# Local attention: the order of the projections, and which PSUM banks they use

## The reference, cut to what matters

```
q, k, v = split(layernorm(x) @ w_qkv.T + b_qkv)      # 16 heads of 16
scores  = q @ k.T / 4, for keys within 16 tokens of the query (window 33)
context = softmax(scores) @ v
x       = x + context @ w_out.T + b_out
```

## Time and profile before

| | us |
|---|---|
| timed runs | 1705.42, 1699.30, 1704.94 |
| their median | 1704.94 |
| the profiled execution | 1711.97 |
| its span, first to last instruction | 1709.9 |

### The profile page before, as it was taken

The page is one execution under the profiler, slowest core; times in us unless marked ns, Lnnn a source line. Parts: engine busy times, 40 slices in busy tenths (PEclk is TensorE's granted clock), DMA queues, the critical chain, the costliest instruction groups (busy, mean ns, idle before and its releaser), DMA issues.

```text
span 1709.9 us, 41993 instructions
## 1 busy us (share of the span) xinstructions
PE 1623.2 (95%) x14962; PEld 1099.3 (64%) x14963; DVE 1146.7 (67%) x2505; ACT 856.6 (50%) x1474; POOL 671.8 (39%) x652
## 2 busy tenths in 40 slices
PE   6999999999989999998999999999999989997999
PEld 3565556666656776765555656666566767776666
DVE  6677765666656666657765556666687677776675
ACT  4355533444376655644344334443466565564774
POOL 2342332334213222232332323444244588888243
PEclk9999999999999999999999999999999999999999
DMA  7132323333301211003210123333332033221011
GB/s 253 50 103 80 104 79 94 110 111 108 86 18 26 37 25 25 1 1 96 84 42 28 42 70 103 111 111 93 93 67 44 7 71 77 58 59 40 14 37 50
DMA packets 90149, 115.69 MB, mean 68 GB/s; under 512 B 9296, under 2 KB 76400, under 8 KB 90032
## 3 DMA queue, kind: packets, MB, share of 16 engines
q1 hardware_dynamic: 69680, 71.17, 14.8%
q0 software_dynamic: 20352, 42.88, 8.8%
HBM read 66.11 MB, written 47.90 MB: 67 GB/s over the span
## 4 chain that ended last, share of the span: by engine, by line
PE 78%; DVE 7%; POOL 4%; ACT 4%; issue 4%; DMA 2%; another core or an unknown queue 1%; SPq 0%; DVEq 0%; ACTq 0%; POOLq 0%
PE ps L1701 17%; PE ps L1703 17%; PE ps L1702 17%; PE ps L1944 3%; PE ps L1945 3%; PE ps L1717 2%; PE ps L1925 2%; PE ps L1926 2%; PE ps L2041 2%; PE ps L1882 2%; PE ps L1863 2%; PE ps L2200 2%; PE ps L2182 1%; PE ps L2170 1%; PE ps L2006 1%
## 5 line engine op out<-in xcount | busy, mean ns | idle before, releaser
L719 POOL DMA_INDIRECT routed<-work x142 | 136.1, 959 | 235.4 <-DVE work L1456 230.3
L1701 PE MATMUL ps<-later_hi,work 128*128 (+1 forms) x632 | 202.6, 321 | 1.3 <-ACT work L1054 1.0
L1703 PE MATMUL ps<-later_hi,work 128*128 (+1 forms) x632 | 202.7, 321 | 0.0
L1702 PE MATMUL ps<-later_lo,work 128*128 (+1 forms) x632 | 202.7, 321 | 0.0
L1701 PE MATMUL ps<-xt_hi,wsh 128*128 128x512 f16 x512 | 194.8, 381 | 5.6 <-DVEq L1205 2.3
L1702 PE MATMUL ps<-xt_lo,wsh 128*128 128x512 f16 x512 | 194.6, 380 | 0.0
L1703 PE MATMUL ps<-xt_hi,wsh 128*128 128x512 f16 x512 | 194.5, 380 | 0.0
L864 ACT ACTIVATE work<-ps 128x512 f32<-128x512 f32 x128 | 76.4, 597 | 180.3 <-PE ps L1703 170.4
L650 POOL TENSOR_TENSOR rstd<-mv,eps 128x4 f32<-128x4 f32 x49 | 14.7, 300 | 386.7 <-DVE mv L1149 375.3
L1701 PE MATMUL ps<-wsh,work 128*128 128x256 f16 x512 | 140.9, 275 | 3.8 <-ACT work L853 2.7
L1703 PE MATMUL ps<-wsh,work 128*128 128x256 f16 x512 | 140.9, 275 | 0.0
(11 more groups left out here) (247 smaller groups left out, 4206.5 us busy)
## 6 DMA issues: line engine op xcount, KB each, us to landing
work<-expert_x SPq DMA_DIRECT2D x142, 129.0 KB
yg<-in_w_later SPq DMA_DIRECT2D x9, 496.0 KB
w1q<-in_w_later SPq DMA_DIRECT2D x9, 496.0 KB
yg<-in_w SPq DMA_DIRECT2D x8, 512.0 KB
values<-wsh SPq DMA_DIRECT2D x8, 512.0 KB, 3.4
later_hi<-values SPq DMA_DIRECT2D x16, 256.0 KB, 4.7
later_lo<-values SPq DMA_DIRECT2D x16, 256.0 KB, 4.9
out_x<-x SPq DMA_DIRECT2D x8, 512.0 KB, 3.0
```

Of the source, the lines that this page charges most:

```text
L719: nc.gpsimd.indirect_dma_start(routed[:, :], bass.IndirectOffsetOnAxis(m.homes[:, i:i + 1], 0), m.t_y[:, i % 4, :], None).then_inc(s[f"til ...
L1701: nc.tensor.matmul(out_, a[0], b[0], start=start, stop=False)
L1702: nc.tensor.matmul(out_, a[0], b[1], start=False, stop=False)
L1703: return nc.tensor.matmul(out_, a[1], b[0], start=False, stop=stop)
```

## The change

Nothing that is computed changes. The banks are given out anew, and the filling work is cut in two.

- Banks: 0 and 1 hold the projections, with the two changed over (the first query projection in 1, the second in 0, and so on); 1 and 2 the transposed rows at t=2; 3 and 4 the scores; 5 and 6 the turned probabilities; 7 all contexts, except tile 2 of the last sequence, which has bank 2.
- The transposes at t=2 now wait for all copies of query and key projections but the last.
- A context waits until the one just before it has been read by VectorE (before: the one before that).
- The filling work of a tile is cut in two parts, one ahead of the scores and one behind: one query or key projection, half of the values, half of the output projection. The second half of the values waits for the transposed rows to be read (before: both).

```diff
-        WXT = 4
+        WXT = 5
+        WXT_AMID = 1
+        WTURN = 5
+
+        def context_bank(g, t):
+            return 2 if is_last(g) and t == 2 else 7
...
                     for j in js:
-                        if j == 0 and (not isinstance(g, int) or g):
-                            if not isinstance(g, int) or g >= 3:
-                                pe.wait_ge(s["y_taken"], 2 * (g - 2))
+                        if j < 2 and g:
+                            if g >= 3:
+                                pe.wait_ge(s["y_taken"], 2 * (g - 2) - 1 + j)
                             else:
                                 pe.wait_ge(s["v_copied"], g * HALVES)
...
-                            ins = mm3(ps[:, j % 2, :], both(aqkv, slice(c, c + P)), xt(u, k), k == 0, k == KT - 1)
+                            ins = mm3(ps[:, 1 - j % 2, :], both(aqkv, slice(c, c + P)), xt(u, k), k == 0, k == KT - 1)
...
-                def values_rows(g, u):
-
-                    if isinstance(g, int) and g == 0:
-                        pe.wait_ge(s["qk_copied"], 2 * KT)
-                    else:
-                        xt_ready(g + N0(n) + 1)
-                    for half in range(HALVES):
+                def values_rows(g, u, halves=range(HALVES)):
+
+                    for half in halves:
+                        if half == 0:
+                            pe.wait_ge(s["qk_copied"], (g + 1) * 2 * KT)
+                        elif not is_first(g):
+                            xt_ready(g + N0(n) + 1)
...
-                    if has_turn(g, t, 2):
+                    if is_last(g) and t >= 2:
                         pe.wait_ge(s["ct_lo"], g * TPS + t - 1)
+                    elif has_turn(g, t, 1):
+                        pe.wait_ge(s["ct_lo"], g * TPS + t)
...
+                def rows_part(g, u, t, part):
+                    if t < 2 and not is_last(g):
+                        queries_keys(g + 1, 1 - u, (2 * t + part,))
+                    elif t == 2 and not is_last(g):
+                        values_rows(g + 1, 1 - u, (part,))
+                    elif t == 3 and has_turn(g, 0, 1):
+                        project(g - 1, 1 - u, (part,))
 
                 def step(g, u):
                     for t in range(TPS):
                         if t == 2 and not is_last(g):
-                            pe.wait_ge(s["qk_copied"], (g + 2) * 2 * KT)
-                            transposes(g + N0(n) + 2)
+                            if is_first(g):
+                                pe.wait_ge(s["bias_row"], 1)
+                            pe.wait_ge(s["qk_copied"], (g + 2) * 2 * KT - 1)
+                            transposes(g + N0(n) + 2, b=WXT_AMID)
                         if has_turn(g, t, 2):
                             g2, _, t2 = turns_back(g, u, t, 2)
                             turn(g2, t2)
                         if has_turn(g, t, 3):
                             context(*turns_back(g, u, t, 3))
+                        rows_part(g, u, t, 0)
                         if t < TPS - 1:
                             scores(g, u, t + 1)
                         elif not is_last(g):
                             scores(g + 1, 1 - u, 0)
-                        if not is_last(g):
-                            if t < 2:
-                                queries_keys(g + 1, 1 - u, (2 * t, 2 * t + 1))
-                            elif t == 2:
-                                values_rows(g + 1, 1 - u)
-                        if t == 3 and has_turn(g, 0, 1):
-                            project(g - 1, 1 - u)
+                        rows_part(g, u, t, 1)
```

More of the change, by code:

```diff
@@ L1648, in take @@
                         xs = x[:, ds(g * TPS + 2 * half, 2), :]
-                        nc.vector.scalar_tensor_tensor(out=xs, in0=ps[:, half, :].rearrange("p (t d) -> p t d", t=2),
+                        nc.vector.scalar_tensor_tensor(out=xs, in0=ps[:, 1 - half, :].rearrange("p (t d) -> p t d", t=2),
                                                        scalar=1 / WS, in1=xs, op0=ALU.mult, op1=ALU.add).then_inc(s["y_taken"], 1)
@@ L1659, in step @@
                             dve.wait_ge(s["bias_product"], 1)
-                            nc.vector.scalar_tensor_tensor(out=bo_row, in0=ps[:, 7, 0:D], scalar=1 / WS, in1=bo_row,
+                            nc.vector.scalar_tensor_tensor(out=bo_row, in0=ps[:, 2, 0:D], scalar=1 / WS, in1=bo_row,
                                                            op0=ALU.mult, op1=ALU.add).then_inc(s["bias_row"], 1)
@@ L2141, in value_bias @@
                         own = tuple(b[:, f:f + 1].broadcast_to([P, P]) for b in m.bv)
-                        ins = mm3(ps[:, 7, 0:D], own, both(ao, slice(f * D, (f + 1) * D)), f == 0, f == KT - 1)
+                        ins = mm3(ps[:, 2, 0:D], own, both(ao, slice(f * D, (f + 1) * D)), f == 0, f == KT - 1)
                     ins.then_inc(s["bias_product"], 1)
-                def values_rows(g, u):
-                    if isinstance(g, int) and g == 0:
-                        pe.wait_ge(s["qk_copied"], 2 * KT)
-                    else:
-                        xt_ready(g + N0(n) + 1)
-                    for half in range(HALVES):
+                def values_rows(g, u, halves=range(HALVES)):
[4 more added lines that the diff above has]
+                            xt_ready(g + N0(n) + 1)
                         for t in range(2 * half, 2 * half + 2):
@@ L2199, in context, with project @@
                             own = m.vz[u][:, t * BPT + blk].rearrange("p a (d e) -> p (a d) e", e=KT * 4)[:, :, f * 4 + h]
-                            ins = nc.tensor.matmul(ps[sl, 6 + t % 2, f * P + blk * QB:f * P + (blk + 1) * QB], own, m.pt[:, t % 2, j, sl],
+                            ins = nc.tensor.matmul(ps[sl, context_bank(g, t), f * P + blk * QB:f * P + (blk + 1) * QB], own, m.pt[:, t % 2, j, sl],
                                                    start=True, stop=True, skip_group_check=True)
                     ins.then_inc(s["c_ready"], 1)
-                def project(g, u):
+                def project(g, u, halves=range(2)):
                     pe.wait_ge(s["ct_hi"], (g + 1) * TPS)
@@ L2211, in project @@
                         pe.wait_ge(s["v_copied"], (g + 3) * HALVES)
-                    for half in range(2):
+                    for half in halves:
                         for t in range(2 * half, 2 * half + 2):
@@ L2215, in project @@
                             for f in range(KT):
-                                ins = mm3(ps[:, half, (t % 2) * D:(t % 2 + 1) * D], (m.c_hi[:, u, f, sl], m.c_lo[:, u, f, sl]),
+                                ins = mm3(ps[:, 1 - half, (t % 2) * D:(t % 2 + 1) * D], (m.c_hi[:, u, f, sl], m.c_lo[:, u, f, sl]),
                                           both(ao, slice(f * D, (f + 1) * D)), f == 0, f == KT - 1)
                         ins.then_inc(s["y_ready"], 1)
+                def rows_part(g, u, t, part):
[5 more added lines that the diff above has]
+                        project(g - 1, 1 - u, (part,))
                 def step(g, u):
```

23 lines of the change are left out of this document (12 added, 11 removed).

## The result

Twenty-two timed runs of each kernel give a median of 1699.88 us after the change (1696.16 to 1703.79) and 1704.0 before (1697.72 to 1706.67). The ratio is 0.998, with a 95% interval of 0.9972 to 0.9988: the change makes the kernel faster by 0.2%, some 4 us. The forecast was 1700.7 us and -4.2. Timed again at the end of the experiments, beside the kernel before, the same kernel had 0.9969 (0.9955 to 0.9982).

What follows compares the result with a forecast made beforehand. The loop was taken to be held by GpSimd's chain from masking to the first turn, then TensorE and VectorE work. Six loops -3.7 us and the start -0.5 gave -4.2, from 1704.94 to 1700.7 us; range 1695 to 1707.

Steps and rivals of the forecast that it cites:

- The loop: Local attention, VectorE's masking of one sequence's first scores to the next's: 15.04 + 6.95 + 3.88 + 0.1 = 25.97 us.
- the transposes' wait: Transposes at t=2 lose their 0.78 us wait for ScalarE's copy; loop 4 gains 0.31, not 0.95 us.
- the changes of kind: TensorE's extra switches between large and small matmuls in each tile: 0.1 us a loop, bounds 0 and 0.4.
- The gaps: TensorE's 0.5 to 1.1 us stops within scores, for instruction fetch, vanish; wins 0.7 us in each of loops 1-3.
- One bank for contexts: Each context waits for VectorE's subtraction of the one before; the next context is 3 us or more behind: costs nothing.
- the scores' delay of 1.3 us: Half a projection ahead of the scores: they end 3.7 us after context start, against VectorE's 3.88; hidden by 0.2 us.
- The take: VectorE's take of the output half frees bank 1 2.0 us after the first turn; projection wants it at 2.1: hidden.
- The start of the stage: First transposes of local attention go some 0.4 us earlier, and the chain to the turn moves with them: -0.5 us.
- Rival 1: Gaps within scores stay, 0.6 us each in loops 1-3, 0.8 in 4-6: 1704.9 us; chance 0.19.
- rival 2: Gaps hit the third and fourth tile's scores in each loop: +4.2 us, 1709.1 us; chance 0.06.
- Rival 3: TensorE, 24.88 us busy a step, becomes the bound: six loops save 10.3 us, 1694.7 us; chance 0.08.
- Rival 4: Transposes still wait, for scale or the third copy: -2.4 instead of -4.2 us, 1702.5 us; chance 0.12.

Runs made afterwards that it cites:

- The second edit on GpSimd's row: Changed kernel with GpSimd's first-tile normalize ahead of scale, transposes behind the third tile's context, split behind its copy: ratio 0.9938 to before, six loops 153.10 us.
- the version with both edits: Changed kernel with GpSimd's reciprocal standard deviation first and normalize ahead of scale, transposes and split later: 0.9928 to before, again 0.9933; six loops 151.57 us.
- the next edit: Changed kernel with GpSimd's reciprocal standard deviation made ahead of the first tile's maximum subtraction: ratio 0.9972 to before, six loops 154.81 us.

## Why the prediction was right

The mechanism was right, and the size of the whole came out closer than its parts: 3.3 us were won in the loops instead of 3.7, 0.2 at the start instead of 0.5, and 0.2 to 0.6 at the end, where nothing was forecast. That -4.2 meets the measured -4.1 so closely is in part luck. Step by step, in its own order:

- *The loop.* Reckoned 15.04 + 6.95 + 3.88 + 0.1 = 25.97, measured 15.04 + 7.07 + 3.88 = 25.99 in loop 4. Six loops: 155.8 reckoned, 156.2 measured.
- *Only 0.31 of the 0.95 us of the transposes' wait is won.* The turn now waits for GpSimd, 0.42 or 0.43 us in each of loops 2 to 6 and 0.11 in loop 1, a little under the 0.5 to 0.7 that was named as the sign. Loop 4 is 0.19 us shorter (0.31 less the changes of kind); put back alone, the late transposes cost 0.44 a loop. The second edit on GpSimd's row confirms that this row held the loop: with the normalize one place further ahead, the loops fall by 0.5 us each. I had taken the whole row as fixed, though, and its first part wasn't: there VectorE's sum stood just behind.
- *The gaps vanish with half a projection in between.* Shown from both sides: old order on new banks has them, new order on old banks has none. The price of 0.7 us in each of loops 1 to 3 was read from loops that differ in other things too: loop 1 has the stretch at half clock, in loop 2 VectorE stops for 0.50 us between its statistics, in the changed kernel as well. And "in 40 tiles" should be the stage's 32.
- *The changes of kind cost 0.1 a loop.* Visible now: from the last matmul of 256 columns to the scores it is 0.20 us (1475.60 to 1475.80), to the next one like it 0.11. There is one such place in the 7.07 (the other, before 1481.85, is hidden by VectorE's work). Of the 0.12 over 6.95, 0.10 is in these scores, 1.19 from start to start (1475.80 to 1476.99) where it was 1.10, and 0.02 in the two halves. The kernel without the halves has loops 5 and 6 shorter by 0.1.
- *One bank for contexts costs nothing, the scores' delay of 1.3 us is hidden by 0.2 us.* Both hold; the kernel with all filling work ahead shows that the cover ends where it was reckoned.
- *The take is hidden by 0.1 us.* Nearly: two waits, 0.5 us in all. In two of the experiments, all filling work ahead and halves on the old banks, it grew to 3.4 and 3.2 us.
- *The start of the stage.* Reckoned -0.5 us; from A(0) to A(1) it went from 23.60 to 23.44, so -0.2. The transposes there now wait 0.73 us for GpSimd's scale. This and 0.4 us of loops is the part of the sum that was too good; the end of the stage, reckoned at nothing, gave 0.6 us back (36.11 to 35.47 from A(7) to the next sublayer), and 0.2 in the second profile of the changed kernel (35.89), so how much of it is chance stays open.

Rival 1 (gaps stay) and rival 2 (two gaps a loop) fall with the missing gaps. Rival 3 (TensorE the bound) is nearly reached by the version with both edits only, with loops 2 to 6 of 25.1 to 25.5 against 24.88 us of busy time. Rival 4 fails, as the transposes wait in no loop; they wait for the scale only at the start.

## What to carry to other kernels

When a wait is taken away in a pipeline of several engines, follow the loop from one point through all engines back to the same point: what is won is what the removed wait stood above the next latest arrival, here 0.3 of 0.95 us as reckoned, and 0.2 to 0.4 as measured. An engine whose operations stand back to back may still have only a small lead over another; the reckoning that predicted the change to 0.5 us was off by four fifths for the next edit, since it didn't ask which operand each piece of the row would wait for if it came earlier. And where TensorE stops within a long run of very small matmuls, try parting it by large ones, if these are there to be moved.

## What the runs showed of the hardware

- TensorE can stop in the middle of 64 small matmuls when these follow 64 others, 128 in 2.2 us with as many weight loads. The idle time is 0.3 to 1.0 us. It lies at a fixed place in the instruction list and moves with instructions that do nothing.
- Before each such break a packet of 16 KB of the instruction queue starts, in the kernel before 2.4 to 2.8 us ahead of the end of the break (the earlier trace rows is one). The end of the break follows the end of the packet: the packets themselves took 0.9 to 1.45 us, and in all 21 idle stretches of TensorE in this stage that a profile here marks "issue", in five of the kernels, it goes on 1.2 to 1.5 us after its packet has ended. That the break is the wait for this packet fits all of it; no run changed the fetch itself, so that much is argued.
- A packet close to a context isn't enough for a break. In the kernel before, packets at 1484.23 and 1510.48 start within 0.1 us of a context, the scores stand right behind it, and there is none; why isn't known. In the changed kernel packets start 0.1 to 0.2 us behind a context at 1421.24, 1447.57 and 1499.39, as before the breaks of sequences 4 to 6 (0.1 to 0.2 us), and there, with half a projection ahead of the scores, none follows either.
- The statement of the Trainium skill, "Runtime: NRT & Kernel Launch", section "Instruction fetch mechanics", that crossing a block is mostly hidden, holds for the other crossings here: there are five packets in a step, and one break.
- 64 fulfilled waits moved the break by 16 float32 matmuls, and each step moves it by 9 (after 37, 46 and 55 in sequences 4, 5 and 6). How instructions are counted there stays open.
- At the start of loop 1, near a turn before which TensorE had stood idle for 2.7 us, its granted clock is 0.5 for 3.4 us in the kernels before and after. The kernel with both edits has one profile with such a stretch and one without; with it the loop is 1.2 us longer (25.31 against 24.13).
- In the changed kernel loops 2 and 5 are 0.2 to 0.4 us longer than their neighbours, in both of its profiles. In loop 2 VectorE stands idle for 0.50 us between its statistics, which the profile puts down to the statistics themselves. In loop 5 VectorE has a short break in its own list, between them:

```profile
1508.76 0.25 DVE L1154 BATCH_NORM_AGGREGATE mv<-stats 128x2 f32<-128x6 f32 x2
1509.17 0.25 DVE L1154 BATCH_NORM_AGGREGATE mv<-stats 128x2 f32<-128x6 f32 x2 [0.16 <-issue]
```

It was seen and not tested.
